# Eight blocks chained on one core: reciprocals, reload of x, experts' weights and opening placed anew

## The reference

```python
x = x + tanh(g_xattn[i]) * xattn_i(layernorm(x), ctx_2048, ...)    # i = 0..3
x = x + tanh(g_ffn[i])   * ffn_i(layernorm(x), ...)
```

## Time and profile before

| | |
|---|---|
| runs | 3059.21, 3059.64, 3060.09 us |
| the profiled execution | 3059.54 us, its span 3057.8 us |
| TensorE, busy share of the span | 86% |
| VectorE, ScalarE, GpSimd | 57%, 39%, 30% |
| mean granted clock of TensorE | 0.932 |

### The profile page before, as it was taken

How to read it: one execution, slowest core, us unless ns; L and a number is a source line. 1 busy time by engine, 2 the same in 40 slices (tenths; PEclk the granted TensorE clock), 3 DMA queues, 4 the chain that set the end, 5 groups by cost and what they waited for, 6 DMA issues and landing times. The chain is left out here.

```text
span 3057.8 us, 36158 instructions
## 1 busy us (share of the span) xinstructions
PE 2632.1 (86%) x11447; PEld 1671.9 (55%) x11447; DVE 1753.8 (57%) x3263; ACT 1196.7 (39%) x2550; POOL 930.9 (30%) x434
## 2 busy tenths in 40 slices
PE   7998799788887679999959998738699998699898
PEld 3555487655434456656546553426476653477555
DVE  2444576467765989989377664512277773444221
ACT  0222222267743688788014555111125553222111
POOL 0222000066732110010015775033318982322122
PEclk9998899899988889999979999869899999799999
DMA  9663113665403410100063421074465430212722
GB/s 278 223 241 139 55 62 124 182 166 142 111 1 114 165 56 28 46 37 28 14 170 107 132 68 29 1 288 110 106 183 172 121 102 1 84 41 71 262 56 47
DMA packets 137548, 333.52 MB, mean 109 GB/s; under 512 B 18608, under 2 KB 21681, under 8 KB 133041
## 3 DMA queue, kind: packets, MB, share of 16 engines
q1 hardware_dynamic: 110192, 262.71, 27.7%
q0 software_dynamic: 12864, 29.06, 4.1%
q10 hardware_dynamic: 14336, 39.85, 3.9%
HBM read 237.24 MB, written 97.72 MB: 110 GB/s over the span
## 5 line engine op out<-in xcount | busy, mean ns | idle before, releaser
L1982 POOL TENSOR_TENSOR L_attn_total<-L_attn_total,L_attn_probs 128x2048 f32<-128x2048 f32 x103 | 471.8, 4581 | 31.6 <-ACT L_attn_probs L1910 22.1
L2016 DVE TENSOR_REDUCE L_attn_row_max<-L_attn_rows_ps 128x1 f32<-128x512 f32 x512 | 338.9, 684 | 149.6 <-PE L_attn_rows_ps L1776 145.5
L1910 ACT ACTIVATE L_attn_probs<-L_attn_s_ps 128x512 f32<-128x512 f32 x512 | 288.0, 601 | 269.1 <-PE L_attn_s_ps L1797 264.2
L521 PE MATMUL L_ffn_hidden<-L_ffn_x_high,L_ffn_up_high 128*128 128x512 f32 x688 | 295.9, 430 | 73.2 <-DVE L_ffn_routes L432 25.8
L1797 PE MATMUL L_attn_s_ps<-L_attn_q_stack,L_attn_k_stack 98*128 98x512 f32 (+1 forms) x768 | 311.7, 432 | 21.1 <-ACT L_attn_probs L1910 20.7
L398 ACT ACTIVATE L_ffn_sums<-sims 128x128 f32<-128x128 f32 x1024 | 314.5, 389 | 29.0 <-DVE L_ffn_routes L418 22.3
L521 PE MATMUL L_ffn_hidden<-L_ffn_x_low,L_ffn_up_high 128*128 128x512 f32 x688 | 272.8, 397 | 0.0
L1776 PE MATMUL L_attn_rows_ps<-L_attn_k_stack,L_attn_q_stack 96*128 96x512 f32 x512 | 223.1, 439 | 23.0 <-DVE L_attn_row_max L2016 17.1
L542 PE MATMUL L_ffn_y<-L_ffn_down_in,L_ffn_h 128*128 128x512 f32 x512 | 230.8, 596 | 1.9 <-DVE L_ffn_h L649 1.9
L1797 PEld LDWEIGHTS L_attn_s_ps<-L_attn_q_stack,L_attn_k_stack 98*128 98x128 f32 (+1 forms) x768 | 145.7, 194 | 158.1 <-ACT L_attn_probs L1910 73.3
L1910 ACT ACTIVATE L_attn_probs<-L_attn_s_ps,keep_mask 128x512 f32<-128x512 f32 x256 | 183.8, 783 | 82.8 <-DVE L_attn_s_ps L2028 82.4
(11 more groups left out here) (310 smaller groups left out, 4526.2 us busy)
## 6 DMA issues: line engine op xcount, KB each, us to landing
L_attn_k_stack<-k_parts SPq DMA_DIRECT2D x144, 256.0 KB, 4.8
L_attn_q_stack<-q_parts SPq DMA_DIRECT2D x72, 256.0 KB, 6.0
k_parts<-L_attn_stage SPq DMA_DIRECT2D x32, 512.0 KB, 2.8
L_attn_abs_in<-in_L_ffn_w SPq DMA_DIRECT2D x12, 1024.0 KB, 10.8
L_attn_kv_parts<-L_attn_part ACTq DMA_DIRECT2D x12, 1024.0 KB, 4.8
L_attn_ctx<-ctx_parts SPq DMA_DIRECT2D x24, 512.0 KB, 9.3
L_attn_wv<-L_attn_kv_parts SPq DMA_DIRECT2D x24, 512.0 KB, 7.1
q_parts<-L_attn_stage SPq DMA_DIRECT2D x24, 512.0 KB, 3.6
```

The source lines that it names most:

```text
L521: last = nc.tensor.matmul(hidden_ps[0:m, b, side, :], w[:, i, e0:e0 + m], x_parts[xp][:, i, h * HALF:(h + 1) * HALF], start=(q == 0), stop ...
L1910: nc.scalar.activation(probs[:, g % P_SLOTS, h, :], s_ps[:, v % S_SLOTS, :], ACT.Exp, **kinds).then_inc(exp_done, 1)
L1982: nc.gpsimd.tensor_tensor(total[:], first, probs[:, g % P_SLOTS], ALU.add).then_inc(added, 1)
L2016: nc.vector.tensor_reduce(row_max[:, hq, i:i + 1], rows_ps[:, r % R_SLOTS, :], AX_X, ALU.max, negate=True).then_inc(max_done, 1)
```

## The change

- Third attention: the row products of units 0 to 23 are placed by a table, up to two in a unit; the reciprocals are eight of 64 columns, from unit 10 on; `NORM_KT` is 5 there. The opening has another order, and the statistics made in the sublayer before are used.
- Fourth attention: x is reloaded from `x_sums` by SP at its start and no more at the end of the routed block; the statistics (item S) come behind K00 K01 V00 V01 W0 W1 of a new opening order.
- Second attention: the mask is loaded and made in the attention's own block.
- First attention: `wo` and `bo` are loaded into the tiles of `wv` and `bv` when the values are done, before the block ends.
- Third feed-forward: experts 0 and 1 are loaded in the norm's block, experts 2 to 7 at the start of the routed block, which first waits for the scatters.

```diff
@@ -442,6 +442,7 @@
...
+            env.tile_stats.taken = final
...
         with nc.Block() as block:
             @block.sync
             def _(sp):
+                sp.wait_ge(slots.scattered, 16 * PICKS * TILES)
                 sp.dma_start(sums.rearrange("(t p) d -> p t d", p=P), env.x[:]).then_inc(kept, 16)
...
                 sp.wait_ge(summed, 16 * I)
-                if not last:
-                    for t in range(TILES):
-                        sp.dma_start(env.x[:, t, :], sums[t * P:(t + 1) * P, :]).then_inc(back[t], 16)
...
-                if not last:
-                    for t in range(TILES):
-                        dve.wait_ge(back[t], 16)
-                        env.tile_stats.take(env, dve, t)
-                    env.tile_stats.finish(dve)
...
@@ -1508,9 +1499,11 @@
...
-    INVERT_AT = {u: part for part, u in enumerate((8, 9, 10, 11) if less_max_rows else (4, 6, 7, 8, 9, 10, 11, 12))}
-    INVERTED = SEQ // len(INVERT_AT)
-    NORM_KT = 3
+    invert_units = (10, 10, 10, 14, 15, 16, 17, 17) if made else (8, 9, 10, 11) if less_max_rows else (4, 6, 7, 8, 9, 10, 11, 12)
+    INVERT_PARTS = len(invert_units)
+    INVERT_AT = {u: [part for part, v in enumerate(invert_units) if v == u] for u in invert_units}
+    INVERTED = SEQ // INVERT_PARTS
+    NORM_KT = 5 if made else 3
...
+    ROWS_AT = (2, 2, 1, 2, 2, 1, 1, 2, 0, 1, 1, 1, 0, 1, 1, 1, 1, 1, 2, 1, 0, 0, 0, 0)
+    assert len(ROWS_AT) == JOIN_AT and sum(ROWS_AT) == ROWS - EARLY_ROWS
+
     def rows_at(n, u):
         if not less_max_rows:
             return []
+        if made and u < JOIN_AT and n + 1 < SETS:
+            first = EARLY_ROWS + sum(ROWS_AT[:u])
+            return [(n + 1, first + k) for k in range(ROWS_AT[u])]
         if u >= JOIN_AT:
             return [(n + 2, u - JOIN_AT)] if n + 2 < SETS else []
         if n + 1 == SETS:
...
     if made:
-        order = ("N0 X0 X1 N2 W0 W1 X2 X3 N4 Q00 V00 V01 X4 X5 W2 W3 N6 Q01 V02 V03 X6 X7 Q02 Q03 Q10 Q11 T0 Q12 Q13")
+        order = ("W0 W1 N0 N2 X0 X1 X2 X3 N4 Q00 W2 Q01 W3 V00 Q02 V01 N6 Q03 X4 X5 V02 X6 X7 V03 Q10 Q11 T0 Q12 Q13")
...
+    if x_sums is None:
+        order = "S0 " + order
+    else:
+        order = ("K00 K01 V00 V01 W0 W1 S0 N0 N1 V02 N2 N3 X0 X1 V03 N4 N5 X2 X3 Q00 W2 W3 N6 N7 X4 X5 Q01 X6 X7 K10 K11 "
+                 "Q02 Q03 Q10 Q11 T0 Q12 Q13")
...
@@ -1676,6 +1683,11 @@
...
+                if not less_max_rows:
+                    sp.dma_start(mask_raw[:], io["mask"]).then_inc(mask_loaded, 16)
+                if x_sums is not None:
+                    for t in range(TILES):
+                        sp.dma_start(env.x[:, t, :], x_sums[t * P:(t + 1) * P, :]).then_inc(x_back[t], 16)
...
@@ -1918,13 +1930,16 @@
...
-                act.wait_ge(parts.biases_loaded, 48)
-                if not taken_before:
-                    act.wait_ge(var_done, TILES)
-                nc.scalar.activation(sd[:], meanvar[:, :, 1], ACT.Sqrt, bias=env.eps_ln[:]).then_inc(sd_done, 1)
+                def deviations():
+                    if not taken_before:
+                        act.wait_ge(var_done, TILES)
+                    nc.scalar.activation(sd[:], meanvar[:, :, 1], ACT.Sqrt, bias=env.eps_ln[:]).then_inc(sd_done, 1)
+
                 act.wait_ge(parts.biases_loaded, 48)
                 for item in OPENING:
-                    if item[0] in "KQ":
+                    if item[0] == "S":
+                        deviations()
+                    elif item[0] in "KQ":
                         high_part(item)
...
+                if not less_max_rows:
+                    act.wait_ge(mask_step, 3)
...
@@ -2058,16 +2075,30 @@
...
-                if not taken_before:
-                    for t in range(TILES):
-                        nc.vector.bn_stats(stats[:, t, :], env.x[:, t, :]).then_inc(stats_done, 1)
-                    for t in range(TILES):
-                        dve.wait_ge(stats_done, t + 1)
-                        nc.vector.bn_aggr(meanvar[:, t, :], stats[:, t, :]).then_inc(var_done, 1)
-                dve.wait_ge(sd_done, 1)
-                nc.vector.reciprocal(rstd[:], sd[:]).then_inc(rstd_done, 1)
-                dve.wait_ge(rstd_done, 1)
+                def statistics():
+                    if not taken_before:
+                        for t in range(TILES):
+                            if x_sums is not None:
+                                dve.wait_ge(x_back[t], 16)
+                            nc.vector.bn_stats(stats[:, t, :], env.x[:, t, :]).then_inc(stats_done, 1)
+                        for t in range(TILES):
+                            dve.wait_ge(stats_done, t + 1)
+                            nc.vector.bn_aggr(meanvar[:, t, :], stats[:, t, :]).then_inc(var_done, 1)
+                    dve.wait_ge(sd_done, 1)
+                    nc.vector.reciprocal(rstd[:], sd[:]).then_inc(rstd_done, 1)
+                    dve.wait_ge(rstd_done, 1)
+
+                if not less_max_rows:
+                    dve.wait_ge(mask_loaded, 16)
+                    keep = keep_mask[:, 1, :]
+                    nc.vector.tensor_scalar(keep, mask_raw[:], 0.5, None, ALU.is_gt).then_inc(mask_step, 1)
+                    dve.wait_ge(mask_step, 1)
+                    nc.vector.tensor_scalar(keep_mask[:, 0, :], keep, SCALE, None, ALU.mult).then_inc(mask_step, 1)
+                    dve.wait_ge(mask_step, 2)
+                    nc.vector.tensor_scalar(keep, keep, -1.0, BOUND, ALU.add, ALU.mult).then_inc(mask_step, 1)
                 for item in OPENING:
+                    if item[0] == "S":
+                        statistics()
...
                         if u in INVERT_AT and n:
-                            invert(n - 1, INVERT_AT[u])
+                            for part in INVERT_AT[u]:
+                                invert(n - 1, part)
...
@@ -2240,6 +2273,9 @@
...
+                sp.wait_ge(v_done, CT)
+                sp.dma_start(wv[:], wo_dram).then_inc(env.wo_loaded, 16)
+                sp.dma_start(bv[:], io["bo"].partition_broadcast(P)).then_inc(env.wo_loaded, 16)
...
-def key_mask_block(env, name, keep_mask):
...
-                dve.wait_ge(loaded, 16)
-                nc.vector.tensor_scalar(keep[:], raw[:], 0.5, None, ALU.is_gt).then_inc(step, 1)
-                dve.wait_ge(step, 1)
-                nc.vector.tensor_scalar(keep_mask[:, 0, :], keep[:], 32 ** -0.5, None, ALU.mult).then_inc(step, 1)
-                nc.vector.tensor_scalar(keep_mask[:, 1, :], keep[:], -1.0, 50.0, ALU.add, ALU.mult).then_inc(step, 1)
-                dve.wait_ge(step, 3)
...
-        if early:
+        if weights:
+            wo, bo = weights
+        elif early:
...
-                                           scratch, (wv, bv, wv_loaded), [(io[f"{n}_wkv"], kv_parts[n]) for n in kv_parts])
-                    output_block(env, name, heads_out, gate, env.io["wo"])
+                                           scratch, (wv, bv, wv_loaded), [(io[f"{n}_wkv"], kv_parts[n]) for n in kv_parts],
+                                           env.io["wo"])
+                    output_block(env, name, heads_out, gate, env.io["wo"], early=2, weights=(wv[:], bv[:]))
...
-                        key_mask_block(env, name, keep_mask)
                     parts = AttentionParts(env, name, loads, work, kinds.get("keys_made", False))
-                    streamed_attention_block(env, name, heads_out, parts, keep_mask, env.io["wo"], early, quantised)
+                    streamed_attention_block(env, name, heads_out, parts, keep_mask, env.io["wo"], early, quantised,
+                                             kinds.get("x_sums"))
...
@@ -2809,23 +2824,32 @@
...
-                    def load_all(sp):
-                        for e in range(EXPERTS):
-                            load_up(sp, up_sb, e)
-                            load_down(sp, down_sb, e)
+                    FIRST = 2
+
+                    def load(sp, e):
+                        load_up(sp, up_sb, e)
+                        load_down(sp, down_sb, e)
+
+                    def early(sp):
+                        slots.load_router(env, sp)
+                        for e in range(FIRST):
+                            load(sp, e)
+
+                    def rest(sp):
+                        for e in range(FIRST, EXPERTS):
+                            load(sp, e)
 
                     with nc.sbuf_tensor(f"{name}_xT", [P, DC, TOK], F32) as env.xT, \
                             nc.psum_tensor(f"{name}_logits_ps", [P, HALVES, HALF], F32) as slots.logits_ps:
-                        norm_block(env, name, rows=slots.rows[:, :, 0:D], router=slots,
-                                   early_loads=lambda sp: slots.load_router(env, sp))
+                        norm_block(env, name, rows=slots.rows[:, :, 0:D], router=slots, early_loads=early)
                         expert_weights_block(env, name, shared, normalise, gate, None,
```

(8 more changed lines are left out.)

38 lines of the change are left out of this document (13 added, 25 removed).

## The result

The changed kernel takes 3108.61 us (median of four runs, 3105.62 to 3115.58) against 3059.43: ratio 1.0165, 95% interval 1.0147 to 1.0183, 49 us slower. The forecast was 3081 with a range to 3094: the sign was right, the size not. The profiled execution is the slowest of the four (span 3113.9, time 3115.58), so the whole difference of the two traces is 56 us and not 49; what lies between the stages of the table adds up to nearly nothing.

A forecast was written before the change was run, and what follows sets the result against it. TensorE was busy for 86% of the span, but limits were read stage by stage. The parts, −5.5 − 2.5 − 3 + 23.5 + 0.5 − 3 + 11 = +21 on 3059.6, gave 3081 us; 8-in-10 range 3060 to 3094.

The forecast's parts named there:

- the +21 of the sum: Whole kernel: all parts' gains and losses together, +21 us on 3059.6.
- The late product: Third attention's loop: two more additions put GpSimd's product 37.3 us into a set, against 32.4 where ScalarE wants it.
- TensorE's scores from unit 30 on: Third attention's loop: these stand behind ScalarE's held-up exponentials, so TensorE idles about 8 us in every set.
- the term for the clock: Third attention's loop: half clock behind TensorE's wait, 1.2 us a set taken six times, +7.
- as they overlap I take half, 0.24: 12.7: Third attention's sets: five more row products, 0.24 us each, move the first addition from 11.5 to 12.7 us in.
- −1.8: Third attention's first set: no `normalise` there, and waits for maxima before row products are saved, −1.8 us.
- so 10.6: Third attention's seventh set: first addition moves from 9.43 to 10.6 us in; set of 38.2 against 29.97, +8.2.
- rival (4): Third attention's loop: product isn't late, uneven rows save 1.9 + 1.7 us a set; −24.5, 3035 us; chance 0.11.
- The fourth attention: Its start: block begins earlier, but statistics behind the values delay the first row product to 2252.9; +11 us.
- wait with them: Fourth attention's opening: K10 and K11, which covered the first queries' trip through memory, now carry row products; no separate size.
- The third feed-forward: Its start: scatters without weight loads beside them −4, loads beside the first gathers +1; −3 us (−5 to 0).
- The +1 for loads beside the gathers: Third feed-forward: experts 2 to 7 load beside the first gathers, for which TensorE waits; +1 us.

The follow-up runs named there:

- n4: The changed kernel with `NORM_KT` 4 in place of 5 in the third attention: 3083.67 us, ratio 1.0073.
- n3: The changed kernel with `NORM_KT` back at 3 in the third attention: 3062.69 us, ratio 1.0015.
- b5: The kernel before with only `NORM_KT` set to 5 in the third attention: 3097.93 us, ratio 1.0132.
- n3_rows_old: n3 with the third attention's row products back at one a unit, new reciprocals kept: 3055.75 us, ratio 0.9985.
- carriers: The changed kernel with V02 and V03 moved behind K10 and K11 in the fourth attention's opening: 3105.22 us, ratio 1.0135.
- inv_only: The kernel before with only the third attention's reciprocals in their new places and sizes: 3045.56 us, ratio 0.9958.
- inv_loads: inv_only with the change's expert loads of the third feed-forward: 3046.92 us, ratio 0.9946.
- inv_paced: inv_only with experts 0 to 3 loaded in the norm's block, 4 and 5 in the routing's, 6 and 7 behind two tiles: 3047.51 us, ratio 0.9949.
- loads_old: The changed kernel with all experts of the third feed-forward loaded beside the scatters, as before: 3108.42 us, ratio 1.0162.
- paced: The changed kernel with experts 0 to 3 loaded in the norm's block, 4 and 5 in the routing's, 6 and 7 behind two tiles: 3108.54 us, ratio 1.0163.

## Why the prediction was right in sign and wrong in size

The traces are 35 us further apart than the +21 of the sum: 12 us in the loop (points 1 and 2), 10 in the third feed-forward's tiles (5), 6 in the fourth attention's opening (4), and 6 in two places where kernels without an edit differ as much (7).

1. **The late product (forecast +28 for sets 1 to 7, measured +40).** The reader and the chain of additions were as written: in the second set, which starts at full clock, the product ends 37.8 us in (forecast 37.3), and the turn follows at once. TensorE's wait was 6.7 us and not 8, and began at another instruction than "TensorE's scores from unit 30 on". The steps that failed are terms of the sum. The largest were the uneven rows' (point 2), some 8 of the 12 us. Then the term for the clock, "That is 1.7 us a set; ... I take 1.2, six times": measured it is 1.8 a set in sets 2 to 6, worth 3 us. Of that, 1.2 is the half clock over a set's start, which moves the first addition from 13.2 to 14.3 us on average; 0.6 is the half clock behind the turn, where the next set starts 3.64 us after the turn although its transfers have landed 0.65 earlier, since TensorE is still at the last units. The wait itself doesn't grow from set to set (6.6 to 6.7 in each). n4 and n3 show the steps between: half clock for 6.83 and 0 us, sets of 38 and 34.3.
2. **The uneven rows.** Their prices were all too low. For five more row products ahead of the first addition I wrote "as they overlap I take half, 0.24: 12.7"; at full clock it is 13.2 (0.5 us in each of five sets). In the first set I counted −1.8, and it became 0.7 longer. In the seventh I counted the same 1.2 us ("so 10.6"), and the first addition came 14.95 us in, which makes the set 3.2 us longer than forecast; n3 has 14.7 without the late product, and b5, with even rows, 10.9 and a seventh set of 38.6, where the forecast was 38.2. n3_rows_old shows the uneven rows worth nothing in sets 2 to 6 and 6 us too dear in the seventh.
3. **The reciprocals.** I costed them by busy time (4.3 instead of 3.4 us on an engine with room) and called the difference hidden. They were the best part of the change: 13 us alone. The waits I had put into rival (4), 1.9 us for maxima and 1.7 of clock in a set, were real, and its sum of 3.6 us a set was nearly right (3.0 measured, five sets in 172.1 us against 186.9); only its cause was the place and size of the reciprocals, not the rows. The changed kernel showed none of it, since the late product set the pace.
4. **The fourth attention (forecast +11, measured +17.4).** The first turn of x was forecast 28.4 us into the block and came at 28.7. Behind it the sum was short: it took the stretch to the first row product from before, at full clock, 23.4; it was 25.6, V03 among it in 4.80 us at half clock; and the queries' wait of 7.10 left what follows at half clock for 4 us again. My "wait with them" for K10 and K11 had no price of its own; carriers, which also moves V02 and V03 away from the turns, puts 6 us on both together.
5. **The third feed-forward (forecast −3).** The start gained the 4 us as forecast. "The third expert is wanted only after a quarter of the tiles" was wrong: TensorE waits for expert i at tile i (line 980), though that wait didn't end last. The +1 for loads beside the gathers was the wrong size: adding scatters and gathers share GpSimd's list, so a landing of 7.7 us (2076.53 to 2084.25) instead of the usual 4.8 holds up both. In the traces of the nine kernels with the change's loads the tiles are 5 to 11 us longer than before, in the three with the loads of before about 2; in times, see above.
6. **What held:** the first attention's end, the mask (−2), the third attention's opening (−3.9 for −3), the eighth set. The clash in N0 cost 0.95 us (1.95 against 1.00), not 2; GpSimd's two operations were over at 1546.39, before the later one, L2513, began at 1546.95 and ran its 0.88. By the rule of the Trainium skill, "SBUF — State Buffer", section "Who interferes with whom", a loss needs both engines at work at the same time; the trace agrees, as of the two only L2069 overlapped with GpSimd and only it was longer, by less than the whole of GpSimd's 2.69 us.
7. **What the edits may not explain:** the second attention's first two sets grew by 2.7 us. They are 61.7 to 61.8 in before, b5 and inv_only, and 63.0 to 66.1 in all twelve traces with the mask's edit, but 64.3 and 63.2 in inv_loads and inv_paced too, which have none of the edits there; so whether the mask's edit has a part in it stays open. The fourth attention's second set is 40.1 in the profile before and 41.9 to 44.0 in every other one, with and without edits. One profiled execution of each kernel can't tell such differences from chance.

## What to carry to other kernels

Before an instruction is moved later in an engine's list, find who waits for it and when: here a number changed from 3 to 5 cost 39 us, and the additions between, on an engine that was busy for three quarters of a set, could be read off three rows. A wait on TensorE is to be priced with the half clock behind it, and a long wait with more of it than a short one; in a wait that returns every period, the half clock also delays the start of the next chain. And four instructions among the maxima of an engine with a third of its time free can still hold up TensorE: it was where they stood and how long each was that counted, not their sum.

## What the runs showed of the hardware

- Stretches at granted clock 0.50 around or behind a wait of TensorE: 3.41 us behind one of 3.59, 6.83 in n4 with waits of 2.0 to 2.1, 10.24 and twice 13.65 in the changed kernel with waits of 6.6 to 7.7 us, 2 to 5 us of each stretch in the wait itself. The length doesn't follow the wait alone: the 7.10 us in the fourth attention's opening went with 6.83. The Trainium skill, "TensorE: Matmul & The Clock Gate", Part 1, has a table of two states, 1.2 and 2.4 GHz, and the traces agree: every stretch of every run here, all on one core, is at 0.50 or 1.00.
- A wait in these sets cost more than its length: against n3's 34.3 us, n4's sets are 3.9 longer with 2.0 to 2.1 us of TensorE's waiting, the changed kernel's 8.4 with 6.7.
- Two waits of 0.5 and 1.0 us for a maximum stood in each of sets 2 to 6 of the kernel before. Behind them the clock was at half for 3.41 us in the fourth to sixth (sets of 37.4), for 6.83 in the second (38.8) and not at all in the third (35.9); with 0.5 us in all, in inv_only, there was none in sets 2 to 6.
- Two kernels that differ by 7 to 12 us in one profiled execution had equal medians (loads_old and paced beside the changed kernel); runs of one kernel lie up to 13 us apart here.
